# Source blocks of the 512-wide layer prepared one step ahead, and semaphores cleared in four places

## The reference

```python
h = relu(layernorm(x)); x = x + attention_layer(h)       # heads, batch norms, feed-forward 256-512-256
h = relu(layernorm(x))
h = relu(((1 + eps1) * h + segment_sum(h[src], dst)) @ w1 + b1)   # 256 -> 512
h = relu(((1 + eps2) * h + segment_sum(h[src], dst)) @ w2 + b2)   # 512 -> 512
x = x + ((1 + eps3) * h + segment_sum(h[src], dst)) @ w3 + b3     # 512 -> 256
```

## Time and profile before

| what | us |
|---|---|
| median of three runs | 4454.34 |
| profiled execution | 4454.23 |
| its span | 4452.6 |
| outside the span | 1.6 |
| layer norm stage, in the span | 313.4 to 549.5 |
| wide layer, in the span | 2741.9 to 3867.8 |

### The profile page before, as it was taken

How to read it: one execution, slowest core, us unless ns; L and a number is a source line. 1 busy time by engine, 2 the same in 40 slices (tenths; PEclk the granted TensorE clock), 3 DMA queues, 4 the chain that set the end, 5 groups by cost and what they waited for, 6 DMA issues and landing times. The chain is left out here.

```text
span 4452.6 us, 70250 instructions
## 1 busy us (share of the span) xinstructions
PE 3560.6 (80%) x16469; PEld 2364.4 (53%) x16470; DVE 2157.3 (48%) x7818; ACT 1265.9 (28%) x2537; POOL 2558.3 (57%) x2766
## 2 busy tenths in 40 slices
PE   3876557777777778876999997888888988788887
PEld 1223345555555557764777774444444444466665
DVE  6987667777777773362222221323322232233333
ACT  3972122222222222372333332001111011122222
POOL 5001177777777760035666663677776776477776
PEclk9999967787877789957999998999999999888888
DMA  4432144444444430067888885777777777599999
GB/s 141 173 155 59 49 112 111 112 112 112 112 112 112 112 101 1 29 188 211 244 245 245 244 243 166 223 233 232 235 235 231 234 234 227 181 286 294 296 293 268
DMA packets 388059, 801.61 MB, mean 180 GB/s; under 512 B 81225, under 2 KB 147513, under 8 KB 384614
## 3 DMA queue, kind: packets, MB, share of 16 engines
q0 software_dynamic: 244224, 577.30, 45.9%
q10 hardware_dynamic: 86354, 138.42, 9.7%
q1 hardware_dynamic: 57360, 84.55, 5.8%
HBM read 699.79 MB, written 100.24 MB: 180 GB/s over the span
## 5 line engine op out<-in xcount | busy, mean ns | idle before, releaser
L1702 POOL DMA_INDIRECT l_gathered<-table,record x850 | 809.5, 952 | 375.6 <-issue 245.8
L815 POOL DMA_INDIRECT a_gathered<-table,record x850 | 810.1, 953 | 302.9 <-issue 256.9
L2107 POOL DMA_INDIRECT l_gathered<-table,record x782 | 749.7, 959 | 374.2 <-issue 261.8
L2297 PE MATMUL bank<-l_gathered,l_onehot 128*125 128x512 f32 x1564 | 699.1, 605 | 18.7 <-DVE l_onehot L2152 15.6
L1139 PE MATMUL bank<-a_gathered,a_onehot 128*125 128x264 f32 x1700 | 520.3, 466 | 75.8 <-DVE a_gathered L943 75.7
L2297 PEld LDWEIGHTS bank<-l_gathered,l_onehot 128*125 128x125 f32 x1564 | 301.7, 194 | 397.5 <-issue 382.9
L1804 ACT ACTIVATE l_part<-l_packed 128x1000 fp32r<-128x1000 bf16 (+1 forms) x300 | 314.4, 1072 | 543.3 <-PE bank L1880 378.9
L1139 PEld LDWEIGHTS bank<-a_gathered,a_onehot 128*125 128x125 f32 x1700 | 374.5, 229 | 171.9 <-DVE a_gathered L943 50.8
L1880 PE MATMUL bank<-rows_last,l_part 125*125 125x512 f32 x1250 | 328.0, 426 | 25.1 <-ACT l_part L1804 18.0
L1880 PE MATMUL bank<-rows_first,l_part 125*125 125x512 f32 x1250 | 308.7, 406 | 29.7 <-ACT l_part L1804 29.7
L1899 PE MATMUL bank<-l_gathered,l_onehot 128*125 128x512 f32 x850 | 245.6, 437 | 105.6 <-DMA l_gathered<-table,record 105.4
(11 more groups left out here) (276 smaller groups left out, 5415.6 us busy)
## 6 DMA issues: line engine op xcount, KB each, us to landing
l_packed<-adjacency ACTq DMA_DIRECT2D x201, 250.0 KB, 5.1
adjacency<-d_stage SPq DMA_DIRECT2D x25, 1562.5 KB, 5.2
l_packed<-adjacency ACTq DMA_DIRECT2D x100, 281.2 KB, 5.9
l_gathered<-table,record POOLq DMA_INDIRECT x1632, 4.8
a_gathered<-table,record POOLq DMA_INDIRECT x850
table<-rows_first POOLq DMA_DIRECT2D x50, 250.0 KB
table<-l_work ACTq DMA_DIRECT2D x50, 250.0 KB
l_source_rows<-table ACTq DMA_DIRECT2D x50, 250.0 KB
```

The costliest lines, as they stand in the source:

```text
L815: pool.indirect_dma_start(out=gathered0[s][:, j * TW:(j + 1) * TW], out_offset=None, in_=table0, in_offset=bass.IndirectOffsetOnAxis(ap=re ...
L1702: pool.indirect_dma_start(out=gathered[g][:, j, :], out_offset=None, in_=table, in_offset=bass.IndirectOffsetOnAxis(ap=record[k.t][:, j, 0 ...
L2107: pool.indirect_dma_start(out=gathered[:, j * w:(j + 1) * w], out_offset=None, in_=table, in_offset=bass.IndirectOffsetOnAxis(ap=record[t] ...
L2297: last = pe.matmul(total[0:NB, 0:w], onehot[t][:, j, :], rows[:, j, :], start=False, stop=(j == T - 1), skip_group_check=True)
```

## The change

1. `over_steps` of the wide layer gets a parameter `ahead`. PE keeps 8. DVE and ACT use 9: in step b they prepare source block b + 9, while PE sums block b + 8. The block that PE needs was thus prepared in the step before.
2. In the layer norm stage SP issues the stores of table0 and the two first stores, in place of POOL. SP loads x two steps ahead (lag -2) and stores with lag 3; POOL has no instructions of its own in this stage.
3. Semaphores of set-up, layer norm, attention, feed-forward and mixed layer 0 are not cleared at the end of their stage, and the second meeting of engines there is gone. They are cleared together with those of the next stage that clears: the adjacency stage, the batch norm stage, the wide layer, and mixed layer 2.

```diff
--- before.py
+++ after.py
@@ -152,17 +152,20 @@
         wf1_sb = early_sb("wf1_sb", [P, 2, DFF])
         wf2_sb = early_sb("wf2_sb", [P, 4, D])
 
-        def phase_semaphores(phase):
-
-            taken = []
+        in_use = []
+
+        def phase_semaphores(phase, clear_later=False):
 
             def clear():
-                nc.clear_and_free_semaphores(taken)
+                if clear_later:
+                    return
+                nc.clear_and_free_semaphores(list(in_use))
+                in_use.clear()
                 nc.all_engine_barrier()
 
             def sem(name):
-                taken.append(nc.alloc_semaphore(name))
-                return taken[-1]
+                in_use.append(nc.alloc_semaphore(name))
+                return in_use[-1]
 
             phase.callback(clear)
             return sem
@@ -191,7 +194,7 @@
         tail = arena[:, 8804:8804 + T * REC].rearrange("p (e c) -> p e c", c=REC)
 
         with ExitStack() as phase:
-            sem = phase_semaphores(phase)
+            sem = phase_semaphores(phase, clear_later=True)
 
             loaded = sem("weights_loaded")
             dst_loaded = sem("dst_loaded")
@@ -581,7 +584,18 @@
                         sp.wait_ge(norm_ready[k.s], k.i - 1)
                     sp.dma_start(x_sb[k.t][:, :], block_rows(x, k.b)).then_inc(x_loaded[k.t], 16)
 
-                over_steps(sp, [(load_x, 0)])
+                for s in range(2):
+                    first_store(sp, row_stored[s])
+
+                def store_row(k):
+                    wait_apart(sp, row_ready[k.s], k.i + 2, 2)
+                    sp.dma_start(block_rows(table0, k.b), row[k.s][:, :]).then_inc(row_stored[k.s], 16)
+
+                for b in range(2):
+                    load_x(place(b))
+                over_steps(sp, [(load_x, -2), (store_row, 3)])
+                for s in range(2):
+                    sp.wait_ge(row_stored[s], 16 * (PAIRS + 1))
 
             @block.vector
             def _(dve):
@@ -619,19 +633,6 @@
 
                 over_steps(dve, [(statistics, 0), (normalise, 1), (finish, 3)])
 
-            @block.gpsimd
-            def _(pool):
-                for s in range(2):
-                    first_store(pool, row_stored[s])
-
-                def store_row(k):
-                    wait_apart(pool, row_ready[k.s], k.i + 2, 2)
-                    pool.dma_start(block_rows(table0, k.b), row[k.s][:, :]).then_inc(row_stored[k.s], 16)
-
-                over_steps(pool, [(store_row, 3)])
-                for s in range(2):
-                    pool.wait_ge(row_stored[s], 16 * (PAIRS + 1))
-
             @block.scalar
             def _(act):
                 for s in range(2):
@@ -1531,7 +1532,7 @@
             row_width, kind = 2 * D, F32R
             k_tiles = D // P
             with ExitStack() as phase:
-                sem = phase_semaphores(phase)
+                sem = phase_semaphores(phase, clear_later=(n == 0))
 
                 def pair(name):
                     return [sem(f"l{n}_{name}{s}") for s in range(2)]
@@ -1991,15 +1992,16 @@
                 def total_of(s, i):
                     return tabled_ps[i - (PAIRS - TABLED)] if tabled(s, i) else sum_ps[s]
 
-                def over_steps(engine, stages, beside=None, early=0):
+                def over_steps(engine, stages, beside=None, early=0, ahead=AHEAD):
 
 
                     def step(b, j=0):
                         for stage, lag in stages:
                             if b >= first_step and 0 <= b - lag < BLOCKS:
                                 stage((b - lag) % 2, 2 * j + (b - lag) // 2)
-                        if beside is not None and b < BLOCKS - AHEAD:
-                            beside(b % 2, b % 4, j + (b + AHEAD) // 4)
+                        m = b + ahead
+                        if beside is not None and m < BLOCKS:
+                            beside(m % 2, m % 4, j + m // 4)
 
                     first_step = 0
                     if beside is not None:
@@ -2008,7 +2010,7 @@
                         for stage, lag in stages:
                             if lag == 0:
                                 stage(0, 0)
-                        for m in range(early, AHEAD):
+                        for m in range(early, ahead):
                             beside(m % 2, m % 4, m // 4)
                         first_step = 1
                     for b in range(6):
@@ -2192,7 +2194,7 @@
                                           upper[s][:, :], ALU.subtract).then_inc(lower_ready[s], 1)
                         order.restart()
 
-                    over_steps(dve, [(rounds_of, 0), (finish, 1), (halve, 4)], split_source, 6)
+                    over_steps(dve, [(rounds_of, 0), (finish, 1), (halve, 4)], split_source, 6, AHEAD + 1)
 
                 @block.scalar
                 def _(act):
@@ -2254,7 +2256,7 @@
                     for r in range(2):
                         load_source(r, r)
                     load_parts(0)
-                    over_steps(act, [(load_weights, 0), (copy_turned, 1), (store, 2), (keep_upper, 5)], cast_source, AHEAD)
+                    over_steps(act, [(load_weights, 0), (copy_turned, 1), (store, 2), (keep_upper, 5)], cast_source, AHEAD, AHEAD + 1)
                     for s in range(2):
                         act.wait_ge(stored[s], 16 * (PAIRS + 1))
 
```

## The result

The changed kernel takes 4397.74 us (median of 4 runs, 4394.46 to 4404.07), the kernel before 4455.59 on the same chip (4 runs, 4452.92 to 4461.15): a ratio of 0.987, with a 95% interval of 0.9853 to 0.9887, so 58 us or 1.3% faster. 4403 was forecast, 4385 to 4428 the range. The profiled execution has a span of 4402.5 us, against 4452.6: it was the slowest of the changed kernel's four, so the traces show 50 us of the 58.

A forecast was written before the change was run, and what follows sets the result against it. The prediction took PE, waiting for ACT's cast, to bound the wide layer. Its terms, -44.7 (wide layer), -3.7 (layer norm stores) and -2.6 (clears), summed to -51.0, from 4454.2 to 4403 us; range 4385 to 4428.

The forecast's parts named there:

- PE is the pace-setter before, POOL next.: Wide layer: PE sets the 23.01 us block period; after the change POOL does at 21.78, with PE at 19.5.
- An order problem.: Wide layer: ACT's cast stands behind copies needing PE's work of the same step; PE waits 2.6 us a step.
- Wide layer -44.7: Wide layer: 43 us gained over 35 blocks, 2.9 more at the end, 1.3 lost at the start; bounds -58 and -27.
- POOL's pace: Wide layer: 21.78 us a block, taken from five early blocks where POOL went at its own pace.
- The splits' wait is covered.: Wide layer: DVE's split waits for PE's buffer, covered by 15 us of PE's 34 gather matmuls.
- Layer norm -3.7: Layer norm stage: 4.3 us of POOL's DRAIN gone, 0.6 lost before the first load; between -5 and 0.
- Clears -2.6: Stage ends: five clears and second meetings save 3.8 us, moved clearing costs about 1.2; bounds -1.0 and -4.8.
- a chance of 1%: Rival: something in the merged clears or SP's mixed queue eats the gain; chance 1%.
- The clock rival: Wide layer: waits for gathers lower PE's clock to 0.77, 25.3 us a block, 4529 us in all; chance 5%.
- The lock-out rival: Wide layer: gathers stand for the whole of each DVE instruction, 28 us a block, 4620 us in all; chance 1%.

The follow-up runs named there:

- part 1 alone: The kernel before with only DVE's splits and ACT's casts of the wide layer one step further ahead: 4402.41 us, ratio 0.9874.
- The experiment with DVE alone: The changed kernel with ACT's casts back at eight steps ahead, DVE's splits still at nine: 4743.37 us, ratio 1.0638.
- Alone, part 2: The kernel before with only the layer norm stage's 52 stores issued by SP in place of POOL: 4448.08 us, ratio 0.9974.

## Why the prediction was right

The mechanism of the wide layer was right, by more than one experiment, except for one wait that it took for another; sizes were off by a few us. That the traces show -50.1 in all against a sum of -51.0 is in part luck: the wide layer gave more than its term, the layer norm stage less.

- *PE is the pace-setter before, POOL next.* Right: 1.7 us more of PE's work cost 39 us before and nothing after. PE's own work was forecast as 19.5 us a block and measured as 18.9.
- *An order problem.* Right: part 1 changes nothing but the order of the same instructions on DVE and ACT, and the wait for the cast goes. With DVE's list changed alone it stays. Whether depth in store would help without the order, no run shows.
- *Wide layer -44.7.* Measured -50.0 in the profiled pair, -54.9 for part 1 alone, within the bounds of 27 to 58. The mis-sized term is POOL's pace, 21.78 for 21.56 measured: 35 x 0.22 = 7.7 us. The gathers themselves were longer in the five early blocks of the kernel before than in the steady blocks after (count | busy us, mean ns of one | idle before):

```profile
L2107 POOL DMA_INDIRECT l_gathered<-table,record x86 | 83.9, 976 | 30.7 <-issue 23.8 <-PE bank L2297 6.9
```

```profile
L2109 POOL DMA_INDIRECT l_gathered<-table,record x594 | 574.6, 967 | 181.0 <-issue 166.7 <-PE bank L2299 14.3
```

Of the 30.7 us idle, 4.8 lie ahead of the first gather. From one gather's end to the next one's start it is 0.305 us on average in both stretches, so POOL truly waited for nobody in the early one. Above the common 0.945 us the gathers lose 0.5 us a block there, as the prediction read it, and 0.4 us after. Five blocks are a small sample of that stretching.

- *The splits' wait is covered.* Right here, but for another wait than the one named: the prediction had DVE wait for the buffer that PE frees, and the 26.4 us at line 2168, 0.8 in each of 34 steps, are for ACT's last cast, which frees the one `source_cut`. The experiment with DVE alone shows how dear that wait is uncovered.
- *Layer norm -3.7.* The end gave 4.24, forecast 4.3, the head cost 0.6 to 0.7, forecast 0.6. Alone, part 2 shortens the stage by 3.0. In the changed kernel the stage is only 1.8 shorter, because of the next point.
- *Clears -2.6.* The meetings gave 2.8: five clears and second meetings of 0.5 to 1.2 us, 3.8 together, less 1.0 for longer clears (268 to 765 ns, against the 109 to 394 of the earlier trace rows). What the sum left out is the layer norm stage's body, 2 us longer wherever the clears are merged; the prediction had only a chance of 1% for something of that kind.
- *The clock rival.* PE waits for gathers 1 to 2.6 us at a time in the middle of float32 matmuls, and the granted clock is 0.98 in the steady blocks, as in the early stretch. Between 2940 and 3694 us it fell to 0.50 at 9 of the 26 gather waits longer than 1.5 us, against 25 of the 33 waits for the cast before. The length of the wait alone doesn't decide it: with eight matmuls of zeros a block the same 2.6 us cost the clock 8 times in 31. The Trainium skill's rule in "TensorE: Matmul & The Clock Gate", section "HAM oscillation — how this bites in real kernels" (a wait before each tile sends the array back to half clock each time), held for most of the waits of the kernel before, and for a third of those after.
- *The lock-out rival.* A sixth of DVE's added time reached POOL, so a gather doesn't stand for the whole of that subtraction. Nor for the whole of the rest: DVE works 244.27 / 35 = 7.0 us a block in the changed kernel, and the gathers of a block lose 0.4 us. "SBUF — State Buffer", section "Who interferes with whom", of the Trainium skill has the whole instruction blocked only where DVE is in a mode that uses both ports, and says of `tensor_tensor` that it has no such mode and contends only with what GpSimd reads. So the subtraction done four times doesn't test that rule, and no run here shows whether another instruction of DVE was in such a mode.

## What to carry to other kernels

When the engine that sets the pace waits for another one's small job, look at what stands ahead of that job in its list; if it needs the first engine's work of the same step, putting it ahead of that, which is the same as one step more of lead, removes the wait, but every engine in the hand-over has to move together. Size the gain by the next pace-setter, measured where it truly waits for nobody. Work at a block's end may be moved to another queue only if that queue has the room: check the bytes per block against what it moves with transfers of the same size and shape.

## What the runs showed of the hardware

- POOL's DRAIN behind stores on its queue took 4296 to 4321 ns for 47 to 52 of them, and 8074 to 8548 ns for 93 to 104, and 34 to 58 ns with none. It took that long also when it began 20 and 23 us before the stage's end.
- SP's queue alone moved 123 to 125 GB/s of transfers of 125 rows (128 and 256 KB) between DRAM and the buffers, and 305 GB/s of stores of 1562.5 KB; in the first case POOL's queue beside it brought the sum up to 221.
- Eight matmuls of zeros a block raised the granted clock of the kernel before from 0.94 to 0.98, with the waits ahead of the source sums as long as before, and that of the changed one from 0.98 to 1.00.
- Halving the bytes of a gather left POOL's 0.97 us of work for it as it was; done back to back, gathers stood 0.305 us apart.
